# Softmax sums of an attention stage taken off TensorE: GpSimd and DMA add every key tile into growing sums, and the sums' matmul comes one chunk later

## What is computed

```python
xn = layernorm(x)                                  # x: (2, 2048, 1024) float32
q = (xn @ wq).reshape(b, s, 32, 32)                # 32 query heads of 32
k, v = (xn @ wk), (xn @ wv)                        # 8 key/value heads, each used by 4 query heads
scores = einsum('bihd,bjhd->bhij', q, k) * SCALE   # causal mask
s = einsum('bhij,bjhd->bihd', softmax(scores), v).reshape(b, s, 1024) @ wo
g = silu(xn @ W_base.T + b_base + lora(xn))        # 8 experts, rank 16, the top 2 weighted
out = x + s * g
```

## Time and profile before

| | us |
|---|---|
| median of 3 runs | 3545.49 (3539.39 to 3545.74) |
| the profiled execution: its own time | 3544.42 |
| its span, first to last instruction | 3542.6 |
| `attend`: first score tile to the last sum | 708.7 to 2758.2 |

### The profile page before, as it was taken

The page is one execution under the profiler, slowest core; times in us unless marked ns, Lnnn a source line. Parts: engine busy times, 40 slices in busy tenths (PEclk is TensorE's granted clock), DMA queues, the critical chain, the costliest instruction groups (busy, mean ns, idle before and its releaser), DMA issues. The chain is left out here.

```text
span 3542.6 us, 63490 instructions
## 1 busy us (share of the span) xinstructions
PE 3360.0 (95%) x19200; PEld 2236.6 (63%) x19200; DVE 1873.0 (53%) x4613; ACT 1435.3 (41%) x2658; POOL 1291.0 (36%) x446
## 2 busy tenths in 40 slices
PE   6999999799999999999999999999999799989999
PEld 5888888555555555555555555555554588878887
DVE  5333332567667677667666676677763122223333
ACT  3222221155555556556555565566666110110000
POOL 0000000156666576565565575566667000000000
PEclk9999999699999999999999999999999899999999
DMA  6555544534534444444444444453533444445555
GB/s 224 158 160 179 170 155 133 147 82 106 126 97 112 114 102 108 109 102 116 101 108 115 96 117 110 98 126 98 120 88 93 135 160 144 141 132 178 190 192 175
DMA packets 278980, 461.98 MB, mean 130 GB/s; under 512 B 40352, under 2 KB 156064, under 8 KB 262816
## 3 DMA queue, kind: packets, MB, share of 16 engines
q1 hardware_dynamic: 258960, 328.32, 31.1%
q0 software_dynamic: 16128, 117.45, 14.3%
q10 hardware_dynamic: 3600, 12.58, 1.1%
HBM read 205.03 MB, written 134.74 MB: 96 GB/s over the span
## 5 line engine op out<-in xcount | busy, mean ns | idle before, releaser
L1030 ACT ACTIVATE probs<-cols_ps 128x512 f32<-128x512 f32 x2176 | 1148.8, 611 | 577.5 <-PE cols_ps L977 471.9
L1053 DVE TENSOR_REDUCE row_max<-rows_ps 128x1 f32<-128x512 f32 x1536 | 992.9, 681 | 374.3 <-PE rows_ps L894 372.8
L977 PE MATMUL cols_ps<-q_st,k_st 97*128 97x512 f32 x2176 | 909.3, 427 | 52.3 <-ACT probs L1030 36.3
L894 PE MATMUL rows_ps<-k_st,q_st 96*128 96x512 f32 (+3 forms) x2560 | 900.1, 381 | 28.6 <-DMA q_st<-scratch_q_hi 17.2
L859 POOL TENSOR_TENSOR added<-added,probs 128x2048 f32<-128x2048 f32 x192 | 898.8, 4681 | 26.9 <-ACT probs L1030 21.1
L977 PEld LDWEIGHTS cols_ps<-q_st,k_st 97*128 97x128 f32 x2176 | 412.6, 190 | 399.1 <-issue 221.6
L1057 DVE CUSTOM_DVE_ANT_0 masked_rows<-rows_ps,tri 128x128 bf16<-128x128 f32 (+3 forms) x1024 | 485.9, 484 | 237.2 <-PE rows_ps L894 233.8
L894 PEld LDWEIGHTS rows_ps<-k_st,q_st 96*128 96x128 f32 x2560 | 496.0, 194 | 167.2 <-DVE row_max L1053 69.7
L932 PE MATMUL o_ps<-probs,v_st 128*32 128x512 f32 (+3 forms) x5120 | 539.6, 540 | 2.6 <-ACT probs L1030 2.6
L859 POOL TENSOR_TENSOR added<-probs 128x2048 f32<-128x2048 f32 x48 | 220.0, 4583 | 629.8 <-PE cols_ps L977 614.6
L932 PEld LDWEIGHTS o_ps<-probs,v_st 128*32 128x32 f32 x5120 | 134.9, 110 | 269.1 <-issue 202.4
(11 more groups left out here) (105 smaller groups left out, 3150.4 us busy)
## 6 DMA issues: line engine op xcount, KB each, us to landing
dma_added<-probs POOLq DMA_DIRECT2D x112, 1024.0 KB, 6.9
q_st<-scratch_q_hi SPq DMA_DIRECT2D x128, 256.0 KB, 5.3
x_sb<-in_x SPq DMA_DIRECT2D x32, 512.0 KB, 4.0
scratch_xt_hi<-xt_hi SPq DMA_DIRECT2D x32, 512.0 KB, 6.0
scratch_xt_lo<-xt_lo SPq DMA_DIRECT2D x32, 512.0 KB, 6.8
scratch_q_hi<-out_hi SPq DMA_DIRECT2D x64, 256.0 KB, 2.5
scratch_q_lo<-out_lo SPq DMA_DIRECT2D x64, 256.0 KB, 2.9
q_st<-scratch_q_lo SPq DMA_DIRECT2D x64, 256.0 KB, 4.7
```

Source lines behind the costliest of these rows:

```text
L894: nc.tensor.matmul(rows_ps[rows_slot(k)][:, 0:keys], q_st[c][0:K1, h, i * P:(i + 1) * P], k_st[kbuf][0:K1, CH * p:CH * p + keys], start=Tr ...
L977: ins = nc.tensor.matmul(into, k_st[n.u][:, j * P:(j + 1) * P], q_st[c][:, :, i * P:(i + 1) * P], start=True, stop=not diagonal)
L1030: nc.scalar.activation(probs_of(c, j)[:, :, i * P:(i + 1) * P], cols_ps[cols_slot(AT_T[t])][:, :].rearrange("p (h q) -> p h q", h=NREP), A ...
L1053: nc.vector.tensor_reduce(into, bank[:, :], AX.X, ALU.max).then_inc(rows_free, 1)
```

## The change

`ADDS` and `DMA_ADDS` now take every key tile of every chunk. The first key tile of each list is no longer added: ACT writes it straight into the sum's own buffer (`added[c % 2]`, `dma_added[c % 2]`, two of each), the value product reads it there, and the adds go on top of it once it was weighed. The remaining 33 key tiles of a group go round 11 `probs` buffers. Y has only `added` and `dma_added` to sum (one part for chunk 0), and it stands, with L1 to L4 behind it, right after the first W of the next chunk instead of the last W of its own. The gate's weights are loaded whole (9 pieces of 512 KB) by SP during the last group, where before the next group's q, k and v would have been loaded, and `gate` splits them at its start, ACT copying and DVE subtracting, with TensorE taking both halves of its first tile piece by piece. `PEEL` grows to 3, `l_inv_stored` gets a semaphore for each parity, and O (ACT's copy of `o_ps`) also waits until its buffer was stored.

```diff
-NROWS, NCOLS, NPROBS = 4, 3, 6
+NROWS, NCOLS, NPROBS = 4, 3, 11
...
-ADDS = [[], [0, 1, 2, 3], [0, 1, 3, 5, 6, 8], [0, 1, 3, 4, 6, 7, 9, 11]]
-DMA_ADDS = [[], [], [2, 4, 7], [2, 5, 8, 10]]
-REST = [[j for j in range(TPC * (c + 1)) if j not in ADDS[c] + DMA_ADDS[c]] for c in range(CPB)]
+ADDS = [[0, 1, 2, 3], [0, 3, 5, 6, 7], [0, 3, 5, 6, 8, 9, 10, 11], [0, 3, 5, 6, 8, 10, 12, 13, 14, 15]]
+DMA_ADDS = [[], [1, 2, 4], [1, 2, 4, 7], [1, 2, 4, 7, 9, 11]]
+RING = [(c, j) for c in range(CPB) for j in range(TPC * (c + 1)) if j not in ADDS[c][:1] + DMA_ADDS[c][:1]]
...
+for _c in range(CPB):
+
+    _t = weighed_at((_c + 1) % CPB, 0) + (0 if _c + 1 < CPB else NTG)
     event(_t, "Y", _c)
-    event(_t + 2, "O", _c)
     event(_t + 4, "L1", _c)
...
         def probs_of(c, j):
-            return probs[probs_slot(J_OFF[c] + j)]
+            if j in ADDS[c][:1]:
+                return added[c % 2]
+            if j in DMA_ADDS[c][:1]:
+                return dma_added[c % 2]
+            return probs[probs_slot(RING.index((c, j)))]
...
             def add(n, c, back, j):
                 q0 = max(0, j - TPC * c) * P
...
-                nc.gpsimd.tensor_tensor(added[:, :, q0:CH], other[:, :, q0:CH], probs_of(c, j)[:, :, q0:CH],
+                nc.gpsimd.tensor_tensor(total[:, :, q0:CH], total[:, :, q0:CH], probs_of(c, j)[:, :, q0:CH],
                                         ALU.add).then_inc(pool_added, 1)
...
-                parts = [(probs_of(cc, j), max(0, j - TPC * cc) * P) for j in REST[cc]]
-                if ADDS[cc]:
-                    pe.wait_ge(pool_added, n.lin(NADD, adds_through(cc, NJG) - back * NADD))
-                    parts = [(added, 0)] + parts
+                pe.wait_ge(pool_added, n.lin(NADD, adds_through(cc, NJG) - back * NADD))
+                parts = [added[cc % 2]]
                 if DMA_ADDS[cc]:
                     pe.wait_ge(dma_done, n.lin(16 * NDMA, 16 * (dma_adds_through(cc, NJG) - back * NDMA)))
-                    parts = parts[:1] + [(dma_added, 0)] + parts[1:]
+                    parts.append(dma_added[cc % 2])
...
-            for k in range(NW):
-                act.wait_ge(gw_loaded[k % 2], 16 * (k // 2 + 1))
-                nc.scalar.activation(gw_hi[:, k, :], gw_raw[:, k % 2, :], ACT.Copy).then_inc(gw_hi_ready, 1)
...
+            for k in range(NW):
+                nc.scalar.activation(w_hi[:, k, :], w_raw[:, k, :], ACT.Copy).then_inc(w_hi_ready, 1)
...
+            for k in range(NW):
+                dve.wait_ge(w_hi_ready, k + 1)
+                nc.vector.tensor_sub(w_lo[:, k, :], w_raw[:, k, :], w_hi[:, k, :].bitcast(FP32)) \
+                    .then_inc(w_lo_ready, 1)
```

More of the change, by code:

```diff
@@ L515 @@
 NJG = J_OFF[CPB]
-NVG = NJG // 2
+PER_VISIT = 2
+NVG = NJG // PER_VISIT
 LEAD = 84
@@ L618 @@
 NADD = sum(len(a) - 1 for a in ADDS if a)
-NDMA = sum(map(len, DMA_ADDS))
+NDMA = sum(len(a) - 1 for a in DMA_ADDS if a)
 def adds_through(c, j):
@@ L643, in attend @@
         NL = NREP * CH // P
-        q_st = [sb(f"q_st{i}", [K1 + 1, NREP, CH], FP32R) for i in range(CPB)]
-        k_st = [sb(f"k_st{i}", [K1 + 1, S], FP32R) for i in range(2)]
+        with nc.sbuf_tensor("gw_raw", [P, KT + 1, D], FP32) as gw_raw:
+            pass
+        q_st = [sb(f"q_st{i}", [K1 + 1, NREP, CH], FP32R) for i in range(CPB - 1)]
+        k_st = [sb("k_st0", [K1 + 1, S], FP32R)]
+        sb("gw_raw_end", [P, D])
+        q_st.append(sb("q_st_last", [K1 + 1, NREP, CH], FP32R))
+        k_st.append(sb("k_st1", [K1 + 1, S], FP32R))
         v_st = [sb(f"v_st{i}", [P, S // P, HD]) for i in range(2)]
@@ L648, in attend @@
         probs = [sb(f"probs{i}", [P, NREP, CH]) for i in range(NPROBS)]
-        added = sb("added", [P, NREP, CH])
-        dma_added = sb("dma_added", [P, NREP, CH])
+        added = [sb(f"added{i}", [P, NREP, CH]) for i in range(2)]
+        dma_added = [sb(f"dma_added{i}", [P, NREP, CH]) for i in range(2)]
         row_max = [sb(f"row_max{i}", [P, NREP, TPC, CPB]) for i in range(2)]
@@ L683, in attend @@
         l_inv_ready = sem("a_l_inv_ready")
-        l_inv_stored = sem("a_l_inv_stored")
+        l_inv_stored = [sem(f"a_l_inv_stored{i}") for i in range(2)]
         l_spread = [sem(f"a_l_spread{i}") for i in range(2)]
@@ L687, in attend @@
         o_stored = [sem(f"a_o_stored{i}") for i in range(2)]
-        gw_loaded = [sem(f"a_gw_loaded{i}") for i in range(2)]
-        gw_hi_ready = sem("a_gw_hi_ready")
-        gw_lo_ready = sem("a_gw_lo_ready")
+        gw_loaded = sem("a_gw_loaded")
         NW = KT + 1
@@ L694, in attend @@
         NPAIR = NG // 2
-        PEEL = 2
+        PEEL = 3
         def over_stages(engine, run):
@@ L741, in cols_free_count, with weighed_count @@
             return None if first_group(n) and before < 0 else cols_count(n, before)
[L743 to L747, removed]
+        def weighed_count(n, c, back, j):
+            return n.lin(NVG, visit_of(c, j) + 1 - back * NVG)
         def rows_count(n, ahead, k):
@@ L806, in run @@
                             load_q(n.lin(1, 0 if c == 0 else 1), (c - 1) % CPB)
-                    elif kind == "K" and not last_group:
+                        else:
+                            load_gw(2 * c - 2)
+                            load_gw(2 * c - 1)
+                    elif kind == "K":
                         if not isinstance(n.pair, int) or n.pair > 0 or n.u > 0:
                             wait_apart(sp, values_done, n.lin(NVG, 0), passed)
-                        load_kv(n.lin(1, 1), 1 - n.u)
+                        if last_group:
+                            for k in range(2 * CPB - 2, NW):
+                                load_gw(k)
+                        else:
+                            load_kv(n.lin(1, 1), 1 - n.u)
                     elif kind == "M":
@@ L927, in weigh @@
                         pe.wait_ge(v_loaded[vbuf], n.pair * 16 + 16)
-                pe.wait_ge(probs_ready, made_count(n, cc, back, j0 + 1))
-                for j in (j0, j0 + 1):
+                pe.wait_ge(probs_ready, made_count(n, cc, back, j0 + PER_VISIT - 1))
+                for j in range(j0, j0 + PER_VISIT):
                     q0 = max(0, j - TPC * cc) * P
@@ L1101, in _, with gate @@
             over_stages(dve, run)
-def gate(nc, b_base, sc, w_hi, w_lo, wo, ow_hi, ow_lo):
+        return gw_raw
+def gate(nc, b_base, sc, w_raw, wo, ow_hi, ow_lo):
     ctx = ExitStack()
```

152 lines of the change are left out of this document (78 added, 74 removed).

## The result

The changed kernel takes 3573.8 us in the median (3567.0 to 3582.4) against 3545.6 us: a ratio of 1.008, 95% interval 1.005 to 1.011. It is 0.8% slower, where 3428 us was forecast.

The account below looks back on a forecast made before the run. TensorE's instruction stream plus late `probs` buffers bound the stage. Terms -99 - 53 - 14 + 30 + 5 + 10 + 1 + 3 = -117 took the profiled 3544.4 us to 3427, 3428 us as median; 8-in-10 range 3385 to 3495.

Parts of the forecast that it names:

- first rival: No wait at Y of chunk 3, landings at 6.8 to 7.0 us or TensorE later: 3393 us, chance 0.20.
- -99: Y on TensorE: 7 widths of 512 a group instead of 14, at 0.88 us each, over 16 groups: 99 us saved.
- -53: Waits of TensorE's score matmuls and Y for late `probs` buffers and their DMAs go, except some 5 us: 53 us saved.
- -14: Clock loss behind the wait in even groups goes, 2 us in each of 7 groups: 14 us saved.
- +30: TensorE waits 2 us at Y of chunk 3 for GpSimd's last add, in 15 groups: 30 us lost.
- +5: Groups where the clock drops behind the wait at Y of chunk 3: 5 us lost.
- +3: Last group: Y of chunk 3 waits for the same GpSimd chain, so its saving is lost: 3 us.
- the prediction's own signs: Wrong if Y of chunk 3 waits over 4 us, TensorE's DVE waits grow over 30, or another Y waits for GpSimd or DMA.
- rival 2: Accumulating DMA landings average 8.3 us; Y of chunk 3 waits 4.5 us, clock costs 2 more: 3491 us, chance 0.15.
- Rival 4: Slower: GpSimd's DMA chain decides every group; landings of 9.5 us use up the gain, 10.3 give some 3580 us; chance 0.05.
- DVE, +10: Some time saved at Y comes back as waits for DVE's `rows_ps` banks: 10 us lost in all.
- The rival that let DVE absorb 48 us: DVE absorbs half of what Y frees, 3 us in each of 16 groups: 3466 us, chance 0.13.

Follow-up runs that it names:

- the adds left out: Changed kernel with the store behind the row move and key tiles 11 to 15 of chunk 3 not summed at all: 3399.1 us, ratio 0.958.
- the mended one: Changed kernel with the store behind the row moves, two chunks peeled, key tiles 11, 14 and 15 of chunk 3 on TensorE: 3410.8 us, ratio 0.962.
- Three pairs of runs: Loop turned between chunks 1 and 2 instead of 2 and 3, each against an otherwise equal kernel: 3485.6 for 3506.0, 3410.8 for 3435.7, 3421.6 for 3458.3 us.
- the fourth pair: Changed kernel with only the loop's turn moved back between chunks 1 and 2, against the changed kernel: 3563.2 us, ratio 1.005.

## Why the prediction was wrong

The forecast was -117 us on the profiled execution, which showed +22.6.

**Right: what the change takes off.** Y's 7 widths a group and the waits for `probs` buffers. The stall-free time that the prediction gives under its first rival is 3393 us. The nearest run, with the adds left out, took 3399 us with a dear turn in it; the mended one, 3411 us, has 1.75 widths x 0.88 us x 16 = 25 us of matmuls more than the change asked for, so 3386 without them. The terms -99, -53 and -14 are thus about right in sum; no run here separates the larger ring from the shorter Y. GpSimd is busy for 93.4 and 91.6 us in the two groups shown, where the prediction had 92.

**Wrong, the costliest step: "The new semaphores, the third peeled chunk and O's further wait (the store is some 30 score tiles old) cost nothing".** Two things in it were never looked at. The events that follow Y move eight score tiles later with it, and L4 is one of them: it waits for GpSimd at the head of SP's queue, and behind it stands the row move that chunk 3 cannot start without. I named the store's age for ACT, and not what queues behind the store on SP. Shown by one edit: 68 us. The row move waited 3.8 us in the queue and then stood beside an accumulating DMA. And the loop's turn was taken as free wherever it stands ("the third peeled chunk"). Between chunks 1 and 2 it costs TensorE 2.0 to 3.1 us, between chunks 2 and 3 4.7 to 6.7. Three pairs of runs show it, with 20, 25 and 37 us, by how the waits of the Ys change with it; the fourth pair, 11 us, is within its noise. With the store at 68 and the turn at 20, that is 88 of the 146 us between forecast and result.

**Mis-sized: the wait of Y(3), +30, +5 and +3.** Its mechanism and place were right, the size was not. With the two faults above mended, what relieving GpSimd gives back is 3485.6 - 3410.8 = 75 us, plus the 25 us of matmuls that this costs: 100 us where I had 38. The chain shows where. D(2) issued 2.1 us later than the 11.7 that I read between two edges of the earlier trace rows: key tile 2 was written at 13.1, and the issue came 0.7 us behind it. (In odd groups of the kernel with the store behind the row move it is written at 11.7, as read.) From D(2) to D(11) it took 34.4 us instead of 33.5, because the sum let each DMA issue at the landing of the one before, and in the trace 0.6 us lie between, three times. The last add so ends 2.8 us later than counted, where the whole wait was put at 2: a wait that is the difference of two numbers near 60 us more than doubles with 5% on one of them. In the other groups the gap ahead of Y(3) is 2.8 to 7.0 us, in the last one 16.1, where I had +3; over the 15 groups before the last it averages 4.5. By the prediction's own signs it was wrong: the wait is over 4 us in eight groups. And Y(2), put at nothing with 1.2 us to spare, waits for GpSimd once the store and the turn are mended.

**Wrong rival.** The wait of 4.5 us is the one of rival 2, but it came without rival 2's landings: those in the chain, D(2), D(7) and D(9), average 7.6 us, not 8.3. Rival 4, the only slower one, wanted landings of 9.5 us in the chain. The kernel became slower with a median of 7.8:

```profile
DMA to landing us min/median/max: 6.8/7.8/13.1
```

The long ones are D(11), 9.9 to 13.1 us in the first 15 groups, where it meets the q, k and v loads of the next one, and 6.9 in the last, where there are none. No add waits for it, and moving the k and v loads away brought nothing. The Trainium skill's page "DMA: Bandwidth & Descriptors", section "Issuing engines are not separate DMA queues", says that such transfers interleave on the same engines; the 13.1 beside 6.8 us agree with it, but it is not what decided. (The change adds 80 accumulating DMAs, not the 48 of the prediction: 48 more in all, and 32 that only copied before.)

**The clock.** I gave back 14 us of it and took 5. The mean granted clock of the execution fell from 0.975 to 0.959; it is 0.978 in the mended kernel. It went with the waits, as in the earlier trace rows: over the stage it is 0.96 in the changed kernel, 0.99 in the mended one:

```profile
707.90:2759.20 2051.30, 1889.38 (x10940) 1035.01 (x10938) 1381.75 (x3651) 1210.64 (x2300) 1463.14 (x586) 0.96 0.60 132
```

```profile
714.40:2620.80 1906.40, 1857.04 (x11300) 1026.68 (x11298) 1376.70 (x3651) 1203.24 (x2300) 1402.83 (x542) 0.99 0.61 134
```

A mean of 0.96 is 8% of the stage at 1.2 GHz, some 160 us, and of 0.99 some 40 us. TensorE gets half as far in it, so the difference is worth some 60 us at most.

**DVE, +10.** The waits of score rows for DVE grew from 11.1 to 22.2 us, and are 7.5 in the mended kernel: they came with the waits for `l_few`, not with the denser stream. The rival that let DVE absorb 48 us is refuted.

**What stays open.** Whether it is the accumulating DMA or the loads of q that holds up the instructions at the turn. And whether the store adds anything to the slow landing of the row move: the kernel before shows that the accumulating DMA alone suffices, but one edit took the move away from both.

## What to carry to other kernels

When an event moves, write down for each queue that serves it what it now stands ahead of: the loss here came from a 0.4 us store issue that waited in front of a 0.6 us row move, on an engine that no busy time points to. Then ask what large DMA is under way at the moment at which the small transfer is now issued. An engine that is free for a quarter of the time can still be late at one point, so a sum that another engine waits for should be closed early, with its last few pieces on whoever reads it. Savings measured by two edits add only if they do not remove the same wait.

## What was unexpected in the hardware

The turn of the hardware loop left TensorE idle for at the longest 2.6 to 3.1 us between chunks 1 and 2 and 5.9 to 6.7 us between chunks 2 and 3, with no releaser in the waits; the branch and the late transfer of instructions behind it are in the trace. A move of one shift row, which mostly lands in 1.8 us, took up to 7.3 us beside an accumulating DMA of 1 MB, and in the kernel before it landed only when that DMA had. And an add of 2048 float32 elements on GpSimd took 4.57 us alone and 4.86 to 4.90 right behind a DMA issue of its own queue. "GPSIMD Engine Reference", section 3.1, of the Trainium skill has 4.50 for it, within 2% of the add alone.
